# A mixture-of-experts layer on one core: LayerNorm folded into the first weights, fp16 halves scattered and read back through DMA transposes

## The reference

```python
# attention-like part: differences of neighbouring rows, 8 at a time
normed = diffs / |diffs|;  combined = pos_weights * tanh(2 * |diffs|)
influence = softmax(2 * cos(normed, guidance)) @ guidance
traj = sum(combined * (0.6 * normed + 0.4 * influence)) / sum(combined)
x = layernorm(x + traj)
# router and experts: 8 experts, each row goes to the best one
probs = softmax(x @ Wr + br);  e = argmax(probs);  gate = max(probs)
xn = (x - mean(x)) * rsqrt(var(x) + 1e-5) * ln_g + ln_b
h = relu(xn @ W1[e] + b1[e])          # 128 -> 512
y = (h @ W2[e] + b2[e]) * gate        # 512 -> 128
out = layernorm(x + y)
```

## Time and profile before

| | us |
|---|---|
| median of 3 runs | 222.06 |
| all runs | 220.68, 222.06, 222.31 |
| span of the profiled execution | 219.4 |
| front half, until the last scatter is issued | 120.1 |
| first matmul of layer one | 126.8 |
| first and last start of z's first step | 132.0 and 207.5 |
| last output scatter starts | 212.3 |

### The profile page before, as it was taken

The page is one execution under the profiler, slowest core; times in us unless marked ns, Lnnn a source line. Parts: engine busy times, 40 slices in busy tenths (PEclk is TensorE's granted clock), DMA queues, the critical chain, the costliest instruction groups (busy, mean ns, idle before and its releaser), DMA issues.

```text
span 219.4 us, 5683 instructions
## 1 busy us (share of the span) xinstructions
PE 151.0 (69%) x1395; PEld 125.6 (57%) x1396; DVE 171.0 (78%) x792; ACT 141.9 (65%) x425; POOL 122.4 (56%) x210
## 2 busy tenths in 40 slices
PE   0158975989785989662500199979979979979600
PEld 0014854776664768552400089869869869868500
DVE  2538789878889889986779139989979979989910
ACT  2455619473817386658502288979979979989530
POOL 4322233325728676687777220667767767768670
PEclk9999997585968596655555559999999999999955
DMA  5996760000101010100133211222221221220000
GB/s 154 334 366 190 224 185 0 3 1 0 51 0 38 17 37 14 51 25 25 37 93 106 75 37 28 65 62 56 71 73 52 64 73 54 70 62 23 30 9 0
DMA packets 16409, 15.66 MB, mean 71 GB/s; under 512 B 2810, under 2 KB 13142, under 8 KB 16386
## 3 DMA queue, kind: packets, MB, share of 16 engines
q1 hardware_dynamic: 13458, 10.83, 17.4%
q0 software_dynamic: 2272, 4.27, 5.9%
q10 hardware_dynamic: 656, 0.30, 0.5%
HBM read 10.52 MB, written 5.33 MB: 72 GB/s over the span
## 4 chain that ended last, share of the span: by engine, by line
PE 37%; POOL 18%; issue 13%; DVE 12%; ACT 8%; DMA 5%; DVEq 2%; SPq 1%; ACTq 1%; POOLq 1%
POOL rows L374 12%; PE bank L559 7%; PE bank L545 4%; PE bank L547 4%; PE bank L549 4%; PE bank L548 4%; PE bank L562 3%; PE bank L450 3%; DMA XN<-in_attn_embeddings 3%; PE bank L471 3%; PE bank L518 2%; POOL rstd L362 2%; POOL R L366 2%; ACT sq L578 2%; DVE hl L1006 2%
## 5 line engine op out<-in xcount | busy, mean ns | idle before, releaser
L405 POOL DMA_INDIRECT out<-OUT,tok x39 | 40.5, 1038 | 29.3 <-issue 29.0
L374 POOL DMA_INDIRECT rows<-R,place x32 | 33.9, 1061 | 9.0 <-issue 9.0
L545 PE MATMUL bank<-sel,bias 96*128 (+1 forms) x156 | 35.2, 225 | 5.2 <-issue 5.2
L547 PE MATMUL bank<-xh,W1h 128*128 128x128 f16 x156 | 35.0, 225 | 0.0
L549 PE MATMUL bank<-xh,W1l 128*128 128x128 f16 x156 | 34.8, 223 | 0.0
L548 PE MATMUL bank<-xl,W1h 128*128 128x128 f16 x156 | 34.7, 222 | 0.0
L559 PE MATMUL bank<-W2hl,hh 128*128 x156 | 32.7, 274 | 0.9 <-DVE hl L1006 0.8
L1006 DVE SCALAR_TENSOR_TENSOR hl<-bank,hh 128x512 f16<-128x512 f32 x39 | 26.6, 682 | 6.5 <-ACT hh L682 6.4
L450 PEld LDWEIGHTS bank<-V,C 128*128 128x128 f32 x128 | 24.9, 299 | 11.2 <-issue 11.2
L450 PE MATMUL bank<-V,C 128*128 128x129 f32 x128 | 26.8, 393 | 3.0 <-DVE Y L772 3.0
L562 PE MATMUL bank<-W2hl,hl 128*128 x156 | 28.0, 219 | 0.0
(11 more groups left out here) (162 smaller groups left out, 448.8 us busy)
## 6 DMA issues: line engine op xcount, KB each, us to landing
XR<-rows SPq DMA_DIRECT2D x39, 66.0 KB, 1.8
W<-in_ffn_W SPq DMA_DIRECT2D x1, 2048.0 KB, 11.5
X<-in_attn_embeddings SPq DMA_DIRECT2D x2, 512.0 KB, 9.0
X<-in_attn_embeddings SPq DMA_DIRECT2D x1, 768.0 KB
out<-OUT,tok POOLq DMA_INDIRECT x39, 2.3
XN<-in_attn_embeddings SPq DMA_DIRECT2D x2, 256.0 KB, 8.3
rows<-R,place POOLq DMA_INDIRECT x32, 2.4
C<-in_constants SPq DMA_DIRECT2D x1, 428.0 KB, 4.6
```

What stands on the lines that cost most here:

```text
L374: pool.indirect_dma_start(out=rows[:, :], out_offset=bass.IndirectOffsetOnAxis(ap=place[u % 4][:, k:k + 1], axis=0), in_=R[u % 4][:, k, :] ...
L405: pool.indirect_dma_start(out=out[:, :], out_offset=bass.IndirectOffsetOnAxis(ap=tok[k][:, 0:1], axis=0), in_=OUT[k][:, :], in_offset=None ...
L545: pe.matmul(h, bias3[:, c * P:(c + 1) * P], sel, start=True, stop=False)
L547: pe.matmul(h, wh, xh[k][:, :], start=False, stop=False)
```

## The change

- LayerNorm's scale and shift and the first bias go into W1. For each expert TensorE makes a correction with two matmuls of 512 columns (`fold`: one over W1 itself with a constant stationary tile `Am`, one over b1), and VectorE adds it to W1 times ln_g. This is done for two experts in each of the front iterations 1 to 4, in banks 0 and 1, which `nT_` and `sims` use too. `Am` is made by VectorE in iteration 0 (`stationary`), from ln_g and ln_b.
- The second LayerNorm's scaled row is made in the front half: ScalarE writes `xs` and its fp16 rounding, VectorE the fp16 rest (`rest`), into the scattered row, which now has 264 numbers. GpSimd writes the second scale to a tile r2.
- In the back half SyncE reads the two halves of a block by a DMA that transposes (XT), and the rest of the row by an ordinary one (XR, now 16 buffers). The scaling, the transpose on TensorE, `b_xt`, `b_xh` and `b_xl` are gone, and so are four bias matmuls of layer one.
- Layer two adds both halves of W2 in the same 128 columns, with 13 matmuls of 128 columns, and z is made in one step. The copy `tok` is gone.
- The block loops are written out in full on all engines; waits that the loops left to the order of things are explicit.
- b2 alone is left of the bias tile (128 columns instead of 640).

The diff, cut to its core; the pieces stand in the order SyncE, GpSimd, TensorE, ScalarE, VectorE:

```diff
--- before.py
+++ after.py
-ROW = D + 4
+ROW = 2 * D + 8
+X1 = D
+GATE = 2 * D
+TOKEN = 2 * D + 1
+SIGMA = 4.0
+RN = 16
...
+        FOLD_AT = (1, 2, 3, 4)
...
+            sp.dma_start(b1[:, :], b1_in).then_inc(ld["b1"], 16)
             sp.dma_start(W2[:, :, :, :], w2.rearrange("e (c p) d -> p e c d", p=P)).then_inc(ld["w2"], 16)
...
-            def load(count, k):
-                after(sp, every["z0"], blocks(count(-1), k))
-                after(sp, every["token"], blocks(count(-1), k))
-                sp.dma_start(XR[k][:, :], rows[bass.ds(row[k], P), :]).then_inc(row_loaded[k], 16)
-
-            steps(sp, [(0, load)], load_rows)
+            for j in range(NB):
...
+                if j >= UN:
+                    sp.wait_ge(every["h_ps"], j - UN + 1)
+                sp.dma_start_transpose(XT[k][:, :, :], halves[bass.ds(row[k], P), 0:2 * D]).then_inc(turned[k], 16)
...
+                sp.dma_start(XR[n][:, :], rows[bass.ds(row[k], P), X1:ROW]).then_inc(row_loaded[n], 16)
...
-                pool.wait_ge(s["r2"], u + 1)
+                pool.wait_ge(s["token"], u + 1)
+                pool.wait_ge(s["xl"], u + 1)
...
-                pool.tensor_copy(tok[k][:, :], XR[k][:, D + 2:D + 3].bitcast(I32)).then_inc(every["token"], 1)
...
+            def fold(q):
+                if q == 0:
+                    pe.wait_ge(s["stationary"], 1)
+                    pe.wait_ge(ld["w1"], 16)
+                for h in range(2):
+                    e = 2 * q + h
+                    pe.matmul(c_ps[h][:, :], Am[:, :], W1[:, e, :], start=True, stop=False)
+                    pe.matmul(c_ps[h][:, :], ident[0:E, e:e + 1].to_broadcast([E, P]), b1[:, :], start=False, stop=True).then_inc(s["c_ps"], 1)
...
+                if i - 1 in FOLD_AT:
+                    pe.wait_ge(s["folded"], 2 * FOLD_AT.index(i - 1) + 2)
                 if i < NU:
                     nT_(i)
...
                     infl(i)
+                if i in FOLD_AT:
+                    fold(FOLD_AT.index(i))
...
-                    pe.matmul(h, bias3[:, c * P:(c + 1) * P], sel, start=True, stop=False)
...
-                    pe.matmul(h, wh, xh[k][:, :], start=False, stop=False)
-                    pe.matmul(h, wh, xl[k][:, :], start=False, stop=False)
-                    m = pe.matmul(h, wl, xh[k][:, :], start=False, stop=True)
+                    pe.matmul(h, wh, XT[k][:, 0, :], start=True, stop=False)
+                    pe.matmul(h, wh, XT[k][:, 1, :], start=False, stop=False)
+                    m = pe.matmul(h, wl, XT[k][:, 0, :], start=False, stop=True)
...
-                    pe.matmul(y[:, 0:2 * D], hh[k][:, c * P:(c + 1) * P], w, start=c == 0, stop=False)
...
+                    pe.matmul(y, hh[k][:, c * P:(c + 1) * P], W2hl[:, w, 0:D], start=False, stop=False)
+                    pe.matmul(y, hh[k][:, c * P:(c + 1) * P], W2hl[:, w, D:2 * D], start=False, stop=False)
+                    m = pe.matmul(y, hl[k][:, c * P:(c + 1) * P], W2hl[:, w, 0:D], start=False, stop=c == FC - 1)
...
+            def xs_(u):
+
+                act.wait_ge(s["x1"], u + 1)
+                act.wait_ge(s["r2"], u + 1)
+                if u >= 1:
+                    act.wait_ge(s["xl"], u)
+                for k in range(NT):
+                    a = act.activation(xs[:, k, :], R[u % 4][:, k, X1:X1 + D], ACT.Identity, scale=r2[u % 2][:, k:k + 1], bias=SIGMA)
+                a.then_inc(s["xs"], 1)
+
+            def xh_(u):
+                act.wait_ge(s["xs"], u + 1)
+                act.activation(R[u % 4][:, :, 0:D // 2].bitcast(F16), xs[:, :, :], ACT.Identity).then_inc(s["xh"], 1)
...
-            steps(act, [(5, b_xs), (1, b_hh), (-3, b_fin), (4, b_xt), (-2, b_sd), (4, b_xh)])
...
+            def rest(u):
+
+                dve.wait_ge(s["xh"], u + 1)
+                tt(R[u % 4][:, :, D // 2:D].bitcast(F16), xs[:, :, :], R[u % 4][:, :, 0:D // 2].bitcast(F16), ALU.subtract).then_inc(s["xl"], 1)
...
+            def stationary():
+
+                dve.wait_ge(ld["small"], 64)
+                dve.wait_ge(ld["b1"], 16)
+                ts(b1[:, :], b1[:, :], 1.0 / D, None, ALU.mult)
+                tt(gbA[:, :], gb[:, 1:2], gb[:, 0:1], ALU.subtract)
+                dve.drain()
+                ts(Am[:, :], ones[:, :], gbA[:, 0:1], 1.0 / D, ALU.mult, ALU.mult).then_inc(s["stationary"], 1)
+
+            def fold(q):
+
+                for h in range(2):
+                    e = 2 * q + h
+                    dve.wait_ge(s["c_ps"], e + 1)
+                    stt(W1[:, e, :], W1[:, e, :], gb[:, 0:1], c_ps[h][:, :], ALU.mult, ALU.add).then_inc(s["folded"], 1)
...
+                if i == 0:
+                    stationary()
                 if i >= -1:
                     factors(i)
...
+                if 3 <= i <= NU + 2:
+                    rest(i - 3)
+                if i in FOLD_AT:
+                    fold(FOLD_AT.index(i))
...
-            steps(dve, [(1, b_hl), (-1, b_mv), (0, b_z0), (-2, b_rec), (0, b_z), (-2, b_shift), (0, b_bn), (4, b_xl)])
+            for j in range(-1, NB + 2):
...
+                    stt(z[k][:, :], bank[5 + j % 2][:, 0:D], cg[k][:, :], XR[j % RN][:, 0:D], ALU.mult, ALU.add).then_inc(every["z"], 1)
```

More of the change, by code:

```diff
@@ L78, in constants, with build @@
     return c
[L81 removed]
+def build(nc, x, guide, wr, br, ln_g, ln_b, w1, b1_in, w2, b2, cst, rows, out):
     with ExitStack() as ctx:
@@ L532, in expert_of, with load_experts @@
-            def expert_of(count, k, lead):
-                if isinstance(count(0), int):
-                    return expert[count(0) * UN + k - expert["first"]]
-                return expert[k if k >= lead else UN + k]
-            def b_h(count, k):
-                e = expert_of(count, k, 1)
-                sel = sel16[:, bass.ds(count(0) * UN + k, 1)].to_broadcast([96, P])
-                pe.wait_ge(t["xl"][k], count(1))
+            def load_experts(j):
+                n, half = min(UN, NB - j), (j // UN % 2) * UN
+                pe.load(held_expert[half:half + n], blk_e[0:1, j:j + n])
+                for i in range(n):
+                    expert[j + i] = pe.snap(held_expert[half + i], min_val=0, max_val=E - 1)
@@ L567, in _ @@
+            load_experts(0)
+            for j in range(-1, NB):
+                if 0 < j and j % UN == UN - 2 and j + 2 < NB:
+                    load_experts(j + 2)
+                if j + 1 < NB:
+                    b_h(j + 1)
+                if j >= 0:
+                    b_y(j)
         @block.scalar
```

308 lines of the change are left out of this document (137 added, 171 removed).

## The result

| | before | after |
|---|---|---|
| median (range), us | 221.4 (220.7 to 222.3), 4 runs | 274.3 (274.1 to 274.9), 4 runs |
| ratio, 95% interval | 1 | 1.238 (1.232 to 1.244) |
| span of the profiled execution, us | 219.4 | 272.2 |
| last scatter starts, us | 119.1 | 155.8 |
| z of the blocks, first and last start, us | 132.0 to 207.5 | 166.7 to 260.2 |

The change costs 53 us, where 25 were forecast. The last two lines of the table divide it. The 38 steps from the first z to the last take 93.5 us in place of 75.5, 2.46 a block against 1.99: +18, where -12 was forecast. In between, 2 us are saved (10.9 from the last scatter to the first z, 12.9 before).

What follows compares the result with a forecast made beforehand. No single engine bounds: TensorE and VectorE nearly full in front; TensorE, VectorE, ScalarE in the blocks. Span 219.4 + 38 (front: 8 + 26 + 4) - 12.5 (back) = 244.9, with 2.7 around it about 247 us; range 229 to 264.

Steps and rivals of the forecast that it cites:

- The wait in iteration 0: Front half: VectorE's `stationary` waits for late loads of gb and b1, delaying unit 1's transposes to 26.6 us; +8 us.
- Iterations 1 to 4: Front half: fold and correction close a ring between TensorE and VectorE, 14.6 then 16.6 us each; +26 with ScalarE's share.
- The router's product: Front half, iterations 3 and 4: it comes on top of the 14.6 us ring, adding 2.2 us to the period.
- The rest: Front half, iterations 5 to 9: ScalarE's 2.2 us and VectorE's `rest` remain, partly hidden by GpSimd's backlog; +4 us.
- ScalarE's +4 in the ring: Front half, iterations 3 and 4: `xs` and the rounding put 2.2 us in front of nT's evacuation; +4 us.
- TensorE, 25 x 0.058 = 1.45 us a block: Back half: 25 matmuls of 128 columns, starting every 0.058 us, are TensorE's whole need per block, 1.45 us.
- GpSimd becomes the bound: Back half: GpSimd sets the pace at 1.55 to 1.76 us a block, in place of 1.99; back half -12.5 us together.
- the 1.68: Back half: the time per block taken for GpSimd as the bound, 1.68 us, saving 11.8 us over 38 steps.
- The turn of the loop goes: Back half: a block takes 1.88 us within a turn and 1.99 overall; the rest is the loop's turn, which goes.
- The transposing load costs what the plain one does: Back half: SyncE's transposing load, issued 8 blocks ahead, lands in 1.7 to 3.2 us and so is hidden.
- The rival's forecast of 2.5 to 3.2 us a block: Back half rival: transposing loads pass one at a time and set the pace, 19 to 46 us lost; chance 0.10.
- two times 1309 ns: Back half: 1309 ns per 128x128 DMA transpose, two in a row an estimated 2.6 us a block, about 283 us in all.

Runs made afterwards that it cites:

- a_static: The kernel after, with each block's expert a constant of the program instead of loaded from the table (wrong experts): 265.1 us, ratio to before 1.190.
- a_static_plain: The kernel after, with constant experts and with plain loads in place of the 39 transposing ones: 248.3 us, ratio to before 1.112.
- its four variants: The kernel before with loops written out; that without layer one's bias matmul; that with experts in two pieces; the last with layer one further ahead: 222.3, 219.3, 219.1, 219.2 us.
- b_unrolled: The kernel before, with its engine loops written out and counts as constants: 222.3 us, ratio to before 0.998.
- a_plain: The kernel after, experts still from the table, with plain loads in place of the 39 transposing ones: 272.5 us, ratio to before 1.225.
- a_fourth: The kernel after, with a fourth matmul (zeros times zeros, fixed addresses) in each of layer one's groups: 277.0 us, ratio to before 1.241.

## Why the prediction was right in front and wrong behind

- **The wait in iteration 0, +8**: right. Unit 1's transposes at 26.83 (forecast 26.6), 8.5 late.
- **Iterations 1 to 4, +26**: right in mechanism and sum (+24.6), in part by errors that cancel. The fold's products came 1.06 us apart, the price that was assumed for them. Iteration 1 took 14.8 us (forecast 14.6); iteration 2 took 16.1 (14.6), since VectorE's maxima (2.25) lay in its chain; iterations 3 and 4 took 16.8 and 16.9, where 16.6 and ScalarE's 2.2 make 18.8. The router's product, put at 2.2, is not in the chain (TensorE makes it while it waits for nT), and ScalarE's part is 1.7.
- **The rest, +4**: right in the kernel after (3.5). Together with ScalarE's +4 in the ring the halves were put at 8, and alone they cost 7.9.
- **TensorE, 25 x 0.058 = 1.45 us a block**: this step failed. It took the pitch from the earlier trace rows, the records of a fixed and a repeated address, and multiplied by the number of matmuls; the register instructions between them were given no price, although the program of both kernels shows them. In their place the runs show 0.12 to 0.13 in front of eight matmuls a block that have a fused register instruction ahead, and 2.33 us a block in all; with constant addresses 0.057 (a_static).
- **GpSimd becomes the bound, -12.5**: wrong in consequence. TensorE's queue was the bound, at 2.33. Without it and the transposes the blocks run at 1.77 (a_static_plain), near the 1.68, but that nearness is luck: GpSimd is not in the chain there; TensorE's matmuls and its wait for `hl` make the pace. That VectorE was full in the old blocks at 1.88 was right: 1.89 in the kernel before and its four variants.
- **The turn of the loop goes**: wrong. b_unrolled is the same as before within 0.5%; the load of the table is what stops TensorE, and the kernel after still has it.
- **The transposing load costs what the plain one does**: wrong at its own size. Landing takes 2.4 to 2.5 us in the median and can be hidden, but issuing takes 1.17 us of SyncE's queue, which I had not looked at as a place at all. The rival's forecast of 2.5 to 3.2 us a block was too high (2.24, a_static at some 2.2), and it did not bind, since TensorE's queue was worse: plain loads alone save 1.9 us (a_plain). That the measured 274.3 lies in that rival's 265 to 306 is therefore luck. The Trainium skill's figure in VectorE: DVE Perf Modes (The three transpose paths), two times 1309 ns, would be 2.6 a block; the measured 1.17 for both halves in one transfer decides against adding the two up, as far as issuing goes.

The two halves' errors did not cancel: the front gave its 37 us and the blocks gave 18 more where 12 were to come back.

## What to carry to other kernels

Before matmuls are taken out of a loop, count what else TensorE's queue has to issue: where each address is computed from a register, and TensorE is what holds the pace, a matmul saved is worth 0.01 to 0.02 us and not the 0.058 of its columns, while an added address costs up to 0.07. Where other engines are never idle it is worth nothing; the step between two blocks away from any stop tells the two cases apart, the mean over all blocks does not. Splitting one wide matmul into two to save an addition elsewhere doubles the addresses. And work that is done once but stands in a ring of engines (here 4 iterations x 4.2 us of matmuls and their correction) must be priced by what the ring waits, with the place of its inputs in the load queue as a term of its own.

## What the runs showed of the hardware that was not expected

- A fused register instruction ahead of a matmul (46 to 60 ns in TensorE's queue): 0.12 to 0.13 us between starts in front of L519 and L535 in place of 0.057, for 128 fp16 columns at full clock, and 0.08 in front of L534 behind L536; a single register addition (32 ns, L521) leaves 0.061. An extra matmul with a fixed address in such a group costs 0.01 to 0.02 (a_fourth).
- While the clock is low the queue gets ahead. The kernel after starts its blocks at 161.9 us with matmuls 0.107 apart, at a granted clock of 0.50 (162 to 166 us); from 166.4 on they are 0.057 apart for a dozen matmuls, addresses or not, and then at a clock of 1.00 (168 to 172) 0.12 behind the register instructions. That the queue had filled up in the slow stretch and then ran dry is an inference. A trace's first block thus looks better than the following.
- A transposing load of 128 x 256 fp16 values takes 1.17 us to issue on SyncE and 2.0 to 2.4 behind a load of registers, and its median landing is 2.5 us; the plain load of XR mostly takes 0.36 to 0.44.
- A load of 8 or 9 registers from SBUF stops TensorE for 0.9 to 1.7 us each time, of which the load itself is 0.6 to 1.1.
